# A store moved from ScalarE's queue to GpSimd's queue in a fused scan and quantized feed-forward kernel on eight cores

## The reference

```python
def _bitlinear(x, w):
    return jnp.einsum('bsd,od->bso', _act_quant(x), _weight_quant(w))

# feed-forward block, x is (2048, 2048) for one sequence
h = x * jax.lax.rsqrt(jnp.mean(x * x, axis=-1, keepdims=True) + EPS) * w_norm
gv = _bitlinear(h, w_gv)                 # w_gv: (2 * 8192, 2048)
value, gate = jnp.split(gv, 2, axis=-1)
u = value * jax.nn.silu(gate)
out = _bitlinear(u, w_out)               # w_out: (2048, 8192)
return residual + out

x = _layernorm(x + _L0_attn_ref(x, ...), axis=-1)
x = _layernorm(x + _L0_ffn_ref(x, ...), axis=-1)
```

## Time and profile before

| | us |
|---|---|
| median of the 2 runs (7625.6 to 7632.8) | 7629.2 |
| the profiled execution | 7615.6 |
| its span on the slowest core (core 3) | 7614.0 |
| the fastest core of it (core 6) | 7595.9 |
| the stage of this case, first to last `u_sp` store | 2623.18 |
| the stretch from 4850 us to the end | 2764.00 |

### The profile page before, as it was taken

One profiled execution on the slowest core, in us unless ns is written; L12 is line 12 of the kernel. 1 busy time (PEld: TensorE's weight loads), 2 busy tenths in 40 slices (PEclk: granted clock), 3 DMA queues, 4 the chain that ended last, 5 costly groups with the idle time before them and its releaser, 6 DMA issues.

```text
span 7614.0 us, 49097 instructions; the slowest of 8 cores (7595.9 to 7614.0 us)
## 1 busy us (share of the span) xinstructions
PE 3240.2 (43%) x13138; PEld 1322.2 (17%) x13138; DVE 4175.6 (55%) x3305; ACT 3083.9 (41%) x2970; POOL 315.3 (4%) x599
## 2 busy tenths in 40 slices
PE   2200202102076777767677776000532605245086
PEld 0000000000032333323233332000211202012032
DVE  3845475664744444444444444677776576576712
ACT  3520212122143444444444434366565466465511
POOL 2012000000000000000000000000000000000000
PEclk8555555555588888888888888555766857677587
DMA  8997100001033333333333332111424415233333
GB/s 196 323 337 258 52 22 22 22 22 42 13 130 106 114 111 119 113 116 111 113 114 110 120 107 89 47 59 62 155 83 150 133 58 185 75 121 128 112 122 111
DMA packets 217459, 853.69 MB, mean 112 GB/s; under 512 B 34656, under 2 KB 34656, under 8 KB 159840
## 3 DMA queue, kind: packets, MB, share of 16 engines
q1 hardware_dynamic: 83376, 436.26, 16.9%
q0 software_dynamic: 69296, 246.49, 11.0%
q10 hardware_dynamic: 64512, 167.80, 5.9%
HBM read 694.24 MB, written 167.77 MB: 113 GB/s over the span
## 4 chain that ended last, share of the span: by engine, by line
DVE 49%; ACT 17%; DMA 15%; PE 7%; issue 7%; POOL 2%; ACTq 1%; DVEq 1%; POOLq 0%; SPq 0%
DVE zt L80 16%; DMA ub<-u_sp 5%; DMA qo_sp<-qo_t 4%; DVE res L80 3%; ACT wqt L80 3%; ACT wqs L80 3%; DVE paby L80 3%; DMA wmean<-wgvt 3%; PE pout L1358 3%; DVE Mx L80 3%; DVE gc_t L80 2%; DVE sg_t L80 2%; DVE u_r L80 2%; ACT sg_t L80 2%; ACT gc_t L80 2%
## 5 line engine op out<-in xcount | busy, mean ns | idle before, releaser
L1092 PE MATMUL pvg<-q,qwv 128*128 128x512 bf16 x4096 | 1055.7, 417 | 896.7 <-DVE u_r L80 735.6
L1358 PE MATMUL pout<-q_r,qo_r 128*128 128x512 bf16 x4096 | 910.9, 385 | 1110.4 <-DMA qo_r<-qo_sp 576.3
L80 DVE SCALAR_TENSOR_TENSOR zt<-mq,zt 128x1024 f32<-128x1024 f32 x896 | 1097.6, 1225 | 160.8 <-DVE zt L80 157.7
L80 ACT ACTIVATE mq<-zt,pbh 128x1024 f32<-128x1024 f32 x896 | 1030.0, 1150 | 227.9 <-DVE zt L80 223.5
L1097 PE MATMUL pvg<-q,qwg 128*128 128x512 bf16 x4096 | 925.8, 379 | 0.0
L80 ACT ACT_TABLE_LOAD x81 | 103.9, 1283 | 1675.6 <-DVE q L80 404.3
L1092 PEld LDWEIGHTS pvg<-q,qwv 128*128 128x128 bf16 x4096 | 427.2, 105 | 1494.8 <-issue 1101.2
L1358 PEld LDWEIGHTS pout<-q_r,qo_r 128*128 128x128 bf16 x4096 | 402.8, 99 | 1622.8 <-issue 1161.3
L1097 PEld LDWEIGHTS pvg<-q,qwg 128*128 128x128 bf16 x4096 | 400.8, 98 | 483.2
L80 DVE SCALAR_TENSOR_TENSOR qo_t<-woqt,woqs 128x1024 bf16<-128x1024 f32 x128 | 156.8, 1225 | 505.2 <-DMA qo_sp<-qo_t 334.7
L80 DVE TENSOR_TENSOR ub<-ub,s2b 128x1024 f32<-128x1024 f32 x128 | 156.8, 1225 | 425.9 <-DMA ub<-u_sp 425.2
(11 more groups left out here) (148 smaller groups left out, 3708.5 us busy)
## 6 DMA issues: line engine op xcount, KB each, us to landing
wld<-wgvt SPq DMA_DIRECT2D x128, 1024.0 KB, 4.9
qo_r<-qo_sp SPq DMA_DIRECT2D x128, 1024.0 KB, 5.7
wmean<-wgvt SPq DMA_DIRECT2D x64, 1024.0 KB, 7.3
wmean<-wgvt POOLq DMA_DIRECT2D x64, 1024.0 KB, 11.1
wo_r<-woutT POOLq DMA_DIRECT2D x128, 512.0 KB, 4.1
u_sp<-u_r ACTq DMA_DIRECT2D x64, 1024.0 KB, 3.9
ub<-u_sp POOLq DMA_DIRECT2D x256, 256.0 KB, 5.4
wmean<-woutT SPq DMA_DIRECT2D x64, 512.0 KB, 12.6
```

The lines of the kernel that those rows point to most:

```text
L80: r = f(*a, **kw)
L1092: t.matmul(pvg[:, 2 * q * TS:(2 * q + 1) * TS], qwv[:, r * 2048 + k * 128:r * 2048 + (k + 1) * 128], q1[:, (ts * DC + k) * TS:(ts * DC + k ...
L1358: last = t.matmul(pout[:, d * TS:(d + 1) * TS], qo_r[:, base + d * 128:base + (d + 1) * 128], rhs, start=(j == 0), stop=(j == HC - 1))
```

## The change

The store of `u_sp` and the wait for the `mx` count in front of it leave ACT's list and enter POOL's. POOL's list, until now one loop over the 128 pieces of the second weight matrix, becomes a loop over `j` as on the other engines: the two loads of `wo_r` of the turn first, then the wait for `mx` of chunk `j - 1` and the store. The semaphore, the slots and the counts of the store stay as they are.

```diff
@@ ACT
                     sc.activation(out=gc_t[:],
                                          in_=u_r[:, r * S + ts * TS:r * S + (ts + 1) * TS],
                                          func=AF.Abs)
-                sc.wait_ge(sV.h, TOK[("mx", jj, NTS - 1)])
-                rUSP.inc(jj, sc.dma_start(out=u_sp[jj], in_=u_r[:, r * S:(r + 1) * S]))
             for h in ((0, 1) if j < HC else ()):
                 i = 2 * j + h
                 wl = i % 2
@@ POOL
     @blk.gpsimd
     def _(g):
-        for i in range(2 * HC):
-            if i < 2:
-                g.wait_ge(sV.h, pP_v)
-                g.wait_ge(sA.h, pP_a)
-                g.wait_ge(sLn1.h, tok_ln1_all)
-            else:
-                g.wait_ge(sA.h, TOK[("woq", i - 2)])
-            dg, jw = divmod(i, HC)
-            rWO.inc(i, g.dma_start(out=wo_r[:, (i % 2) * 1024:(i % 2 + 1) * 1024],
-                                   in_=woutT[dg, jw]))
+        for j in range(HC + 1):
+            for h in ((0, 1) if j < HC else ()):
+                i = 2 * j + h
+                if i < 2:
+                    g.wait_ge(sV.h, pP_v)
+                    g.wait_ge(sA.h, pP_a)
+                    g.wait_ge(sLn1.h, tok_ln1_all)
+                else:
+                    g.wait_ge(sA.h, TOK[("woq", i - 2)])
+                dg, jw = divmod(i, HC)
+                rWO.inc(i, g.dma_start(
+                    out=wo_r[:, (i % 2) * 1024:(i % 2 + 1) * 1024],
+                    in_=woutT[dg, jw]))
+            if j >= 1:
+                jj = j - 1
+                g.wait_ge(sV.h, TOK[("mx", jj, NTS - 1)])
+                rUSP.inc(jj, g.dma_start(out=u_sp[jj],
+                                         in_=u_r[:, (jj % 2) * S:(jj % 2 + 1) * S]))
```

## The result

| | before | after |
|---|---|---|
| median, us | 7636.16 (10 runs) | 7481.76 (11 runs, 7444.06 to 7507.75) |
| profiled execution, us | 7615.6 | 7441.98 |
| first to last `u_sp` store, slowest core, us | 2623.18 | 2443.75 |
| mean of its 63 turns, us | 41.64 | 38.79 |

The ratio of the times is 0.9777, with a 95% interval from 0.9752 to 0.9803: the changed kernel is 2.2% faster; whether the gain is more than 2% is not settled, since the interval ends just above 0.98.

What follows compares the result with a forecast made beforehand. It took DVE-ACT hand-overs, held up by the first `qo_sp` store's issue and landing, as the bound. The profiled 7615.6 us less 171, plus 13.6 to the median of two runs, gave 7458 us; range 7441 to 7513.

Steps and rivals of the forecast that it cites:

- The chain: Between chunks, ACT's first `qo_sp` issue, late by a wait and the `u_sp` issue, and its 4.6 us landing hold DVE.
- The 2.71 us a turn: First `qo_t` of a turn starts 2.71 us earlier: 1.16 from ACT being free, 1.55 from the landing leaving the chain.
- 63 x 2.71 = 171 us: Total gain over the 63 turns of the hidden-chunk loop: 171 us.
- the upper end, 180: Gain by the sum of DVE's waits before the first `qo_t`: 334.7 - 154 = 180 us.
- The second store: Second `qo_sp` store of a turn may take 3.83 us; 2.7 us expected, so no cost; up to 49 us otherwise.
- rival (a): Second `qo_sp` store caught behind `u_sp` on the shared DMA engines: up to 49 us, 7507 us; chance 0.17.
- Rival (d): POOL's traffic starves the second `qo_sp` store; turns longer than today from a 6.54 us landing, 7916 us; chance 0.03.
- (b): First `qo_sp` store stays slow with nothing ahead on its queue; only 73 us gained, 7556 us; chance 0.07.
- (c): The change brings nothing because another wait ends at the same moment; 7629 us; chance 0.03.
- (e): POOL's making of descriptors slows DVE, 0.53 us per issue, 34 us in all; 7492 us; chance 0.02.
- POOL's side: POOL issues `u_sp` 0.55 us after its releaser, landing in 4 to 6 us; the added wait and issue cost nothing.
- PE: PE's matmul bursts fill some 30 us of a turn, leaving 8 to 9 us idle; no cost and no gain.

Runs made afterwards that it cites:

- e1: Kernel before without ACT's wait for the last maximum ahead of the `u_sp` store, which stays on ACT's queue; turn 40.87 us, ratio 0.9915.
- e2: Kernel before with four slots for `qo_t` instead of two, so DVE needs no fresh store; turn 39.98 us, ratio 0.9868.
- e3: Kernel before with the first `qo_sp` store issued ahead of `u_sp`, both on ACT's queue, without the wait for the maximum; turn 39.29 us, ratio 0.9803.
- e5: Changed kernel with four slots for `qo_t`, so none waits for a fresh store; turn 38.69 us, ratio to the kernel before 0.9781.
- e6: Changed kernel with POOL holding the `u_sp` store until ACT's first `woqs` is done; turn 38.78 us, ratio to the kernel before 0.9745.
- e9: Changed kernel with one extra 1 MB store on ACT's queue right ahead of the second `qo_sp` store; turn 44.10 us, ratio 1.0216.
- e10: Changed kernel with two extra 1 MB stores on ACT's queue right ahead of the second `qo_sp` store; turn 47.21 us, ratio 1.0522.
- e8: Changed kernel with DVE making the next slice's gate ahead, in a second slot, before `Mx`; turn 34.95 us, median 7212.94 us, ratio 0.9449.

## Why the prediction was right

I forecast 7458 us, 2.2% less, and the ratio of 0.9777 is 2.2% less; 7481.76 is inside the range. That the numbers meet so closely is in part luck. The stage gained 8 us more than forecast, the rest of the span on the slowest core grew by 6 us (4990.9 to 4996.7 us), and the medians of both kernels came out higher than I took them, by 7 us before and 24 us after.

- **The chain** was read rightly. e1 (the wait), e2 (the landing) and e3 (the order) each took the share that the arithmetic of one turn gives them, 0.77, 1.66 and 2.35 us against 0.74, 1.7 and 2.3 expected.
- **The 2.71 us a turn.** All steps stand in the timeline after: issue 0.13 us behind `gc_t`, landing 2.7 us, release by `woqs`. ACT came 0.07 us earlier than forecast, since the issue with nothing ahead took 0.33 us and not 0.40, so DVE's idle time is 2.38 and not 2.45 us.
- **63 x 2.71 = 171 us** was a little low. The idle time before the first `qo_t` fell by 334.7 - 155.9 = 178.8 us and the stage by 179.4: the upper end, 180. I had kept back 10 us for late landings. With 3.0 us of room those landings, up to 6.2 us before and 4.3 us now, matter in only 11 turns.
- **The second store: the mechanism of rival (a) came true, and its price was wrong.** It lands in 4.2 us in the turn shown and 4.4 us in the median, over the 3.83 us that I gave it, and the second `qo_t` waits 38 us more in all. I charged nothing because I took the margin of 1.1 us to be enough; it was not. And I priced the rival at up to 49 us because I took the second `qo_t` to be on the chain as the first is. The step that was wrong is "DVE needs it for the second `qo_t`, at 3570.22. So it may take 3.83 us": the kernel before already shows DVE idle for 3.09 us behind that `qo_t`, waiting for ACT's `wqs`, and ACT does not wait for it. The true room was 3.83 + 2.8. Two errors in opposite directions left the sum unharmed; e5, e6, e9 and e10 show it. Rival (d) had the same fault: it decides not at 6.54 us but, as an estimate, at about 9.3 us (3.83 + 2.8 + the 2.71 gained). On cores 4 and 5 of e9, at 8.1 to 8.5 us, a turn is still shorter than before; on the others, at 11.4 us, it is longer, and e9 as a whole has a ratio of 1.0216 (1.0087 to 1.0345).
- **(b) and (c)** are excluded: the first store landed in 2.7 us, and no other wait on the chain took its place.
- **(e)** is excluded too: `qo_t` and the operations of the last stage still have 1225 ns, with 64 more issues on POOL. The Trainium skill ("GPSIMD Engine Reference", section "Specifications") states a contention with DVE instructions of two SBUF inputs; these runs show none here. DVE is idle when POOL issues the store, but not when it issues the loads of `wo_r`: a `qo_t`, which reads `woqt` and `woqs` in SBUF, runs beside such an issue 62 times before and 110 times after, and takes 1224 to 1228 ns with it and without it. My "with POOL at rest" holds for the first `qo_t` of the earlier trace rows alone; the second, at 3572.93, already ran beside the issue at 3573.31, in the same 1.23 us.
- **POOL's side.** Issue 0.56 us after `Mx` (0.55 forecast), landing 4.1 to 6.8 us, no one waiting for it. Its packets came sooner than I worked out from the `wo_r` load: at the twelfth slice of 0.1 us after the issue and without a pause,

```profile
GB/s 389 389 348 62 0 0 0 0 0 0 0 983 328 0 901 410 0 819 492 0 737 573 0 573 655 82 573 573 164 82 737 492 0 737 573 0 103 369 369 307
```

  where the earlier trace rows have single packets at 1.2 us and the body at 1.8 (the first four slices here are the first `qo_sp` store). So they ran from 3590.2, and with the 2.8 us that they filled before, to about 3593.0: half of the 1 MB was still to come when the second store's packets were due, at 3590.90 + 0.75. That store landed at 3595.1, 1.5 us after the `u_sp` store did. The rule of the Trainium skill ("DMA: Bandwidth & Descriptors", section on queues, rings and completion order), turns between the queue rows packet by packet, gave me hope of nearly no delay; the delay of 1.5 us (4.2 less 2.7) was larger, with `wo_r` in flight as well. Whether the small store stood behind the large one or shared with two others is not settled by these runs.
- **PE** had 556.8 us of idle time in 62 bursts, 9.0 us each, in the forecast 8 to 9.

## What to carry to other kernels

Look at what stands ahead of a small store that someone waits for: 256 KB behind 1 MB on one queue landed 1.9 us later, and giving the small store the head of its queue, with one wait less, took most of the gain without a new engine (e3). Before pricing a delay, follow it past the instruction that waits: if the other engine goes on without it and the next hand-over has idle time, that idle time is room. And when every engine is 40 to 75% busy, look for a hand-over of two engines on one tile; a second slot and one operation moved ahead (e8) were worth more than the change itself.

## What the runs showed of the hardware

- The bytes ahead of a store do not say by themselves when it lands. With one more store of 1 MB in flight beside POOL's 1 MB and 512 KB, the 1 MB store took 9.0 us and the 256 KB store behind it 11.4 us (e9), where 1 MB and the 256 KB behind it took 4.1 and 4.6 us before the change. I had expected 5.0 to 6.5 us. Nor do the transfers of the core itself: on cores 4 and 5 of the same execution, with the same program, the added store took 5.8 us in the median and the one behind it 8.1 to 8.5 us, against 9.2 to 9.7 us and 11.4 to 11.5 us on the other six. In the other timed execution of e9 the spans of these two cores are no shorter than the rest, so it is not a property of the cores; what differed is open.
- A wait that is long met is not quite free: with one more of them in front of `u_r`, DVE's gap there is 0.31 us (e9) and not 0.24. 
- In e8, in which PE stands still least, 16 matmuls take 3.62 us on core 3 and 4.38 us on core 5 at the same time of the run; from 3563 to 3598 us the granted clock is 0.90 on core 3 and 0.78 on core 5. PE is busy 34.86 of these 35 us on core 5 and 30.80 us on core 3. Over the stage the turn is the same within 0.1 us on both; on cores 6 and 7, where the granted clock of the stage is 0.84, it is 35.2 us. So with a granted clock that low PE comes near to being the bound of e8; at 0.92 it is not.
